# Four of 28 node spans: aggregate by gathered rows in the first graph layer as well

## The reference

```python
x0 = x
for l in range(3):                               # GRU layers
    m   = x @ weight[l]
    agg = segment_sum(m[src] * edge_weight[:, None], dst, 6250)
    x   = gru_cell(agg, x, w_ih, w_hh, b_ih, b_hh)
x = layernorm(x0 + x); x1 = x
for W, b in ((W0, b0), (W1, b1), (W2, b2)):      # GIN layers, no weights
    x = relu((x + segment_sum(x[src], dst, 6250)) @ W.T + b)
return layernorm(x1 + x)
```

## Time and profile before

| | us |
|---|---|
| median of 3 runs | 2881.55 |
| the profiled execution | 2883.43 |
| its span in the profile | 2881.7 |
| building stage up to PE's last unit | 993 |
| building stage and tail, up to layer 2's first transposes | 1014.5 |
| layers 2 and 3 up to the GIN layers | to about 2060 |

### The profile page before, as it was taken

One profiled execution on the slowest core, in us unless ns is written; L12 is line 12 of the kernel. 1 busy time (PEld: TensorE's weight loads), 2 busy tenths in 40 slices (PEclk: granted clock), 3 DMA queues, 4 the chain that ended last, 5 costly groups with the idle time before them and its releaser, 6 DMA issues.

```text
span 2881.7 us, 72532 instructions
## 1 busy us (share of the span) xinstructions
PE 2832.6 (98%) x29387; PEld 1881.3 (65%) x29387; DVE 1246.0 (43%) x2716; ACT 947.4 (33%) x1891; POOL 872.5 (30%) x1007
## 2 busy tenths in 40 slices
PE   6999999999999999999999999999999999999998
PEld 5899999999999955555555555555655555555554
DVE  7678877777888514344422344343500010001011
ACT  6777777777777610000001011101400010001111
POOL 4344344443444315554541454544000000000000
PEclk7999999999999999999999999999999999999999
DMA  5666666666662398998996988988487868886884
GB/s 196 267 262 244 245 261 261 257 241 251 262 263 95 113 397 342 350 339 326 355 369 253 340 338 331 357 330 327 149 326 301 310 248 301 309 304 247 318 304 163
DMA packets 134009, 810.64 MB, mean 281 GB/s; under 512 B 17208, under 2 KB 27308, under 8 KB 113948
## 3 DMA queue, kind: packets, MB, share of 16 engines
q1 hardware_dynamic: 111228, 758.32, 67.9%
q0 software_dynamic: 19968, 40.46, 4.4%
q10 hardware_dynamic: 2720, 10.62, 0.9%
HBM read 553.01 MB, written 256.33 MB: 281 GB/s over the span
## 4 chain that ended last, share of the span: by engine, by line
PE 95%; issue 2%; DVE 1%; ACT 1%; DMA 1%; another core or an unknown queue 0%; POOL 0%; DVEq 0%; SPq 0%; ACTq 0%; POOLq 0%
PE ps L969 29%; PE ps L1165 27%; PE ps L1247 19%; PE ps L1240 11%; PE ps L979 1%; PE ps L980 1%; PE ps L1260 1%; PE ps L1261 1%; PE ps L982 1%; PE ps L981 1%; PE ps L1144 1%; ACT ring L1661 0%; DMA sum_rows<-ring 0%; PE ps L1266 0%; PE ps L1267 0%
## 5 line engine op out<-in xcount | busy, mean ns | idle before, releaser
L969 PE MATMUL ps<-ring,Y 128*128 128x448 f32 x2352 | 888.4, 539 | 0.0
L1165 PE MATMUL ps<-ring,Y 128*128 128x448 f16 x4116 | 780.6, 352 | 0.0
L1661 ACT ACTIVATE ring<-ps 128x490 f16<-128x490 f32 (+1 forms) x1344 | 698.3, 651 | 176.7 <-PE ps L1240 169.1
L969 PEld LDWEIGHTS ps<-ring,Y 128*128 128x128 f32 x2352 | 446.4, 190 | 434.8 <-issue 434.8
L1165 PEld LDWEIGHTS ps<-ring,Y 128*128 128x128 f16 x4116 | 402.7, 98 | 373.8
L863 POOL DMA_INDIRECT ring<-y_rows,ring x448 | 431.4, 963 | 518.9 <-PE ps L969 257.7
L1247 PE MATMUL ps<-ring,Y 128*128 (+1 forms) x2744 | 570.2, 360 | 0.4 <-ACT shared L1620 0.4
L1247 PEld LDWEIGHTS ps<-ring,Y 128*128 128x128 f32 x2744 | 503.6, 190 | 8.4 <-ACT shared L1620 0.8
L1240 PEld LDWEIGHTS ps<-shared 64*128 64x128 bf16 x18816 | 320.4, 93 | 76.6 <-issue 59.3
L1240 PE MATMUL ps<-shared 64*128 64x49 bf16 (+1 forms) x18816 | 346.5, 189 | 20.0 <-issue 9.6
L1824 DVE TENSOR_SCALAR ring<-ring 128x128 f32<-128x128 f32 x446 | 130.9, 294 | 388.7 <-DMA ring<-y_rows,ring 205.0
(11 more groups left out here) (196 smaller groups left out, 1450.6 us busy)
## 6 DMA issues: line engine op xcount, KB each, us to landing
ring<-adj_w SPq DMA_DIRECT2D x72, 2688.0 KB
ring<-adj_h SPq DMA_DIRECT2D x42, 2800.0 KB, 9.4
ring<-adj_h SPq DMA_DIRECT2D x42, 2688.0 KB, 9.2
adj_w<-ring SPq DMA_DIRECT2D x48, 2016.0 KB, 11.9
adj_h<-ring SPq DMA_DIRECT2D x56, 1372.0 KB, 5.4
ring<-adj_w SPq DMA_DIRECT2D x24, 2912.0 KB
adj_w<-ring SPq DMA_DIRECT2D x48, 728.0 KB, 6.8
sum_rows<-ring SPq DMA_DIRECT2D x62, 448.0 KB
```

The lines of the kernel that those rows point to most:

```text
L969: mm = pe.matmul(ps[:, bank, 0:GW], Y[:, h, :], slab(s)[:, :, h - h0, :], start=(h == 0), stop=(last and h == TILES - 1))
L1165: mm = pe.matmul(ps[:, par, 0:GW], part[:, h, :], counts_slab(par, s)[:, :, h - h0, :], start=(h == 0 and part is Y_high), stop=(h == TILE ...
L1661: act.activation(strip[:, :, c0:c0 + UNIT * WIN].rearrange("p h (d j) -> p d h j", d=WIN)[:, :, :, w0:w1], psum_unit(a)[:, :, kind, :, :]. ...
```

## The change

The four last spans are no longer aggregated through `add_tiles` in the first GRU layer but by gathered rows, as in layers 2 and 3, during the building.

- Their slots come first (`ORDER`), build counts only (one matmul of three, one eviction of two, two column steps of seven) and have no `add_tiles`. PE's transposes of the inputs move from slots 0 and 1 to slots 1 and 2. The first gates run in slot 6 instead of slot 2.
- In slots 5 to 24 POOL gathers 224 rounds of rows of `x` (11 a slot, 12 in every fifth), ACT multiplies each by the weight two batches later, DVE adds it to the running sum two further batches later, SP stores four rounds at a time between the strips. The 16 row buffers are used in place; before there were 10 for rows and 14 for sums. Slots 26 and 27 fetch the 16 ends.
- Each group of gathers on POOL starts with `batch_begun`, a wait for the first unit of the batch and a `sem_inc`. The near rows are fetched at batch 2 instead of 7, the edge gathers wait for the first unit of batch 3 and 5 instead of the last unit of batch 2 and 4.
- After the last slot PE has the last strip's 49 tiles in six parts, with the gates of five spans between them (before: of one).
- The loops of DVE, ACT, POOL and SP over the slots are written out; the descriptor memory of POOL's DMAs is set to 8192.

```diff
+FIRST_RUN = GATHERS - RUN_SPANS
+ORDER = [*range(FIRST_RUN, GATHERS), *range(FIRST_RUN)]
+GATE_ORDER = [*range(FIRST_RUN - 1), *range(FIRST_RUN, GATHERS), FIRST_RUN - 1]
+SCALE_LAG, SUM_LAG, STORE_LAG = 2, 4, 5
+TAIL_TILES = [0, 6, 15, 24, 33, 42, TILES]
+RUN_SLOTS = range(RUN_SPANS + 1, GATHERS - 3)
+BATCH_ROWS = [2, 2, 1, 1, 2, 1, 0, 2]
-        KEYS_AT, STEPS_AT, LEAPS_AT = 2, 3, 5
+        KEYS_AT, STEPS_AT, LEAPS_AT = 2, 3, 0
-        NEAR_AT = 7
+        NEAR_AT = 2
...
+            def fetch_round(turn, i):
+                if i >= RUN_BUFS:
+                    if i % STORE == 0:
+                        use, q = divmod(i // STORE - STORE_TURNS, STORE_TURNS)
+                        pool.wait_ge(s_stored[q], stored_by(turn, q) + 16 * (use + 1))
+                    pool.wait_ge(s_acc, RUN * turn + i - RUN_BUFS + 2)
+                pool.indirect_dma_start(out=run_bufs[:, i % RUN_BUFS, :], ..., in_=y_rows if turn else x, ...)
+            def batch_begun(n):
+                pool.wait_ge(s_bmm, UNITS * (BUFS + n) + 1)
+                pool.sem_inc(s_mark_pool, 1)
+            def fetch_batch(n):
+                if rounds_at(n) or ends_at(n):
+                    batch_begun(n)
+                for i in rounds_at(n): fetch_round(0, i)
+            def prepare_span(t):
+                fetch_batch(n)
+                pool.wait_ge(s_key, ...); pool.wait_ge(s_colp, t + 1); pool.sem_inc(s_mark_pool, 1)
+                add_own(t + 1, 1 - par)
+                fetch_batch(n + 1)
+                near_rows(t + 3, 1 - par)
+                batch_begun(n + NEAR_AT)
+                gather_near(1 - par)
+                fetch_batch(n + 2)
+                take_places(t + 2, par)
+                batch_begun(n + FETCH_AT[0])
+                gather(par, 0)
+                fetch_batch(n + 3)
+                fetch_batch(n + 4)
+                batch_begun(n + FETCH_AT[1])
+                gather(par, 1)
+                fetch_batch(n + 5)
+                make_columns(t + 1, 1 - par, n + 6)
+                fetch_batch(n + 7)
...
+            def scale_rows(n):                       # ACT, after the evictions of batch n + 2
+                for i in rounds_at(n):
+                    act.wait_ge(s_row[i % RUN_BUFS], 16 * (i // RUN_BUFS + 1))
+                    act.activation(row, row, ACT.Copy, scale=run_edges[:, i, 1:2])
...
+                    sum_batch(n - SUM_LAG)           # DVE, after the one-hots of batch n
...
+            for c, n in enumerate(range(FIRST_RUN - 2, GATHERS)):     # PE, the tail
+                add_tiles(0, TAIL_TILES[c], TAIL_TILES[c + 1])
+                if n < GATHERS - 1:
+                    fused_gates(n)
+                if c < RUN_SPANS:
+                    flip_run(c)
```

More of the change, by code:

```diff
@@ L81 @@
 SPAN = WIN * LANES
+RUN_SLOTS = range(RUN_SPANS + 1, GATHERS - 3)
+BATCH_ROWS = [2, 2, 1, 1, 2, 1, 0, 2]
+MORE_AT, MORE_EVERY = 6, 5
+SLOT_ROWS = [[n + (k == MORE_AT and s % MORE_EVERY == 0) for k, n in enumerate(BATCH_ROWS)] for s in range(len(RUN_SLOTS))]
+assert sum(map(sum, SLOT_ROWS)) == RUN
+ENDS = 2 * WIN * RUN_SPANS
 STRIP_BATCHES = SUB // WIN // BATCH
@@ L844, in _ @@
[L844 to L847 removed]
+            def fetch_round(turn, i):
[4 more added lines that the diff above has]
+                    pool.wait_ge(s_acc, RUN * turn + i - RUN_BUFS + 2)
+                pool.indirect_dma_start(out=run_bufs[:, i % RUN_BUFS, :], out_offset=None, in_=y_rows if turn else x,
+                                        in_offset=bass.IndirectOffsetOnAxis(ap=run_edges[:, i, 0:1].bitcast(I32), axis=0))\
+                    .then_inc(s_row[i % RUN_BUFS], 16)
@@ L849, in _ @@
+            for t in range(GATHERS):
+                prepare_span(t)
             pool.wait_ge(s_steps, WIN * (GATHERS + 2))
@@ L1234, in build_unit @@
                             sums = psum_unit(a)[:, d, :, w - w0, :]
-                            if part == 0:
+                            if not weighted:
+                                rhs = hot[slots, buf, 0, w, 0:TILES]
+                                sums = sums[:, 0, :]
+                            elif part == 0:
                                 rhs = hot[slots, buf, 0:2, w, 0:TILES]
@@ L1251, in add_tiles, with flip_run, state_of @@
                         mm.then_inc(s_fagg, 1)
+            def flip_run(r):
+                n = GATE_ORDER.index(FIRST_RUN + r)
+                pe.wait_ge(s_joined, r + 1)
+                pe.wait_ge(s_fev, START + n)
+                for d in range(WIN):
+                    at = d * LANES
+                    mm = pe.matmul(ps[:, RUN_BANK, at:at + LANES], run_bufs[0:LANES, end_buf(r, d, 0), :],
+                                   ident[0:LANES, 0:LANES], start=True, stop=True)
+                mm.then_inc(s_fagg, 1)
+            def state_of(n):
+                span = GATE_ORDER[n] if isinstance(n, int) else n
+                return xT[:, bass.ds(span * SPAN, SPAN)]
             def fused_rz(n, bank):
-                xg = xT[:, bass.ds(n * SPAN, SPAN)]
+                xg = state_of(n)
                 pe.wait_ge(s_fev, START + n + 1)
@@ L1808, in rounds_by, with sum_row, sum_batch @@
                 return max(0, min(RUN, SLOT_FIRST + SLOT_NEXT * slot))
+            def sum_row(turn, i):
+                done = RUN * turn + i
+                row, last = (run_bufs[:, j % RUN_BUFS, :] for j in (i, i - 1))
+                dve.wait_ge(s_acc, done)
+                dve.wait_ge(s_prod, done - turn)
+                dve.scalar_tensor_tensor(out=row, in0=last, scalar=run_edges[:, i, 2:3], in1=row,
+                                         op0=ALU.mult, op1=ALU.add).then_inc(s_acc, 1)
+            def sum_batch(n):
+                for i in rounds_at(n):
+                    if i:
+                        sum_row(0, i)
             def add_rows(layer, slot, part=range(SLOT_NEXT)):
@@ L2091, in first_columns @@
                 rest = batches(2)
-                for p in range(WPARTS):
+                for p in range(WPARTS if has_weights(0) else 0):
                     part = columns[:, 0, :, 2 + p, :, :]
```

558 lines of the change are left out of this document (303 added, 255 removed).

## The result

| | us, median | lowest to highest | runs |
|---|---|---|---|
| before | 2881.26 | 2879.49 to 2884.94 | 9 |
| after | 2889.52 | 2886.71 to 2892.49 | 9 |

Ratio 1.0028, 95% interval 1.0019 to 1.0037: slower by 8.3 us, more than the 5.8 us that this measurement tells from no change. The forecast was 2920, slower by 38.5. The sign and the range held; the size was 30 us off, and the cause of the loss was not the one forecast. The same file is faster than the kernel before on another chip (third set), so the sign was luck as well.

What follows compares the result with a forecast made beforehand. PE was taken to bound the building stage at 34.2 us a slot; -62.5 us off PE plus 101 us of late columns behind POOL gave +38.5 on 2883.4, 2922, as a median 2920; range 2826 to 2938.

Steps and rivals of the forecast that it cites:

- The saved time: PE's building stage and tail: slot 5 starts at 135, tail 33 us, end at 952 against 1014.5, so -62.5 us.
- ACT and DVE: Scalings add 3.4 us a slot to ACT, sums 3.9 to DVE; both covered, costing nothing by themselves.
- POOL's 35.0: POOL in an 11-round slot: column steps done 35.0 us after PE's first unit, next slot at 38.6 instead of 34.2.
- the +101: Sum of building-stage losses from late columns: 4.4 us in each of 20 slots, plus twelfth rounds and slot 26.
- The price of a gather beside DVE: POOL's building-stage gathers, held up by DVE, take 1.29 us each instead of 0.95.
- The second price: Gap on POOL ahead of a gather behind a wait with `sem_inc`: 0.84 us for eight groups a slot.
- +0.83 count, +2.7 one-hots: DVE after the last column step: a count of 0.83 us and three one-hots of 2.7 before PE's next slot.
- rival two: POOL's gathers held up, but 0.84 paid only after a real wait or another instruction kind: slots 36.3, 2872; chance 0.10.
- Rival one: POOL's gathers not held up by DVE (1.0 each) but keeping their 0.84: slots 35.4, 2853; chance 0.15.
- The forecast's own range: Whole kernel at 2903 to 2937, from slot 5's start and slots of 37.8 to 39.4; chance 0.42.
- The layers kept their pace: Layers 2 and 3 keep pace and chain of ends; smaller stores and in-place buffers within 5 us, taken as nothing.
- some us more or less: Written-out loops: nothing could price them, so some us either way.

Runs made afterwards that it cites:

- third set: Four kernels on chip 11, the kernel before beside them; the changed kernel, unaltered, took 2849.52 us there, ratio 0.9896.
- e1: Changed kernel with layer 1's 224 gathers replaced by POOL clearing the same buffer, chip 10: 2826.59 us, ratio 0.9818.
- e17: The kernel of e15 once more, on chip 14: 2835.69 us, ratio 0.9853.
- e18: The kernel of e16 once more, on chip 14: 2834.60 us, ratio 0.9848.
- e9: The changed kernel, unaltered, once more on chip 11: 2849.52 us, ratio 0.9896 to the kernel before.
- e6: Changed kernel without layer 1's scalings on ACT; sums, gathers and stores stay; chip 5: 2892.98 us, ratio 1.0043.
- e14: Kernel before with two spare gathers a slot behind batch 0's last unit, read by nobody, on chip 7: 2909.97 us, ratio 1.0100.
- e13: The changed kernel, unaltered, once more on chip 7: 2891.01 us, ratio 1.0032 to the kernel before.
- e4: Kernel before with two spare gathers a slot behind batch 0's last unit, read by nobody, on chip 10: 2880.71 us, ratio 1.0005.
- e15: Changed kernel with column steps ahead of batch 5's edge gather (moved to batch 6), rounds redistributed and begun in slot 4; chip 7: 2879.45 us, ratio 0.9999.
- e16: Changed kernel with only POOL's column steps moved ahead of the second edge gather and batch 5's round; chip 7: 2901.01 us, ratio 1.0066.
- e8: Changed kernel with every building-stage group of gathers begun behind its batch's last unit, not the first; chip 5: 2915.64 us, ratio 1.0113.
- first two sets: Sets on chips 10 and 5, four kernels each with the kernel before beside them: gathers, scalings or sums left out, spare gathers, moved work.

## Why the prediction was right or wrong

**The saved time was right.** Slot 5's first added tiles are at 136.41; less the 2.9 us that two batches of units take in a full slot, it counts as started at 133.5 (forecast 135). The tail took 32.3 us (33). 1015.84 less the 64 us of losses is about 952 (952). That is a subtraction; `e1`, which has no gathers of rows at all, has its first transposes of layer 2 at 957.1, so the term is 57 to 63 us (62.5). `e17` and `e18` end the stage at 965.1 and 966.0: their slots with rounds lose nothing, but slot 5's tiles start 4.5 to 4.9 us later than in `e9` (141.1 and 141.5 for 136.6), with one wait of 10.9 us for DVE ahead of it; the rest I did not take apart. Slot 25, without rounds, is 34.3.

**ACT and DVE: right.** A scaling takes 437 ns, not 300, and by `e6` it is covered. Sums take 361 (352), and DVE's own time stays inside the slot. Group by line, 170 to 900 us (count, busy, mean ns, idle before):

```profile
L898 POOL DMA_INDIRECT run_bufs<-in_x,run_edges x212 | 258.6, 1220 | 138.9 <-PE ps L1333 93.9 <-issue 42.5 <-DVE shared L2213 0.3
L1768 ACT ACTIVATE run_bufs<-run_bufs,run_edges 128x128 f32<-128x128 f32 x215 | 82.1, 437 | 0.0
L1960 DVE SCALAR_TENSOR_TENSOR run_bufs<-run_bufs,run_edges 128x128 f32<-128x128 f32 x216 | 77.9, 361 | 6.7 <-ACT run_bufs L1768 3.3
```

**The failed step is POOL's 35.0, and with it the +101.** Columns came at 31.4 us on the recorded chip, where PE lost 1.1 us to them between 170 and 940 us, and at 31.2 on chip 11. The price of a gather beside DVE was about right: 1.220 on average, where 1.29 was taken. The second price was not: I charged 0.84 ahead of each of eight groups, from one row with a real wait and one behind another kind of instruction. In the slot of `e9` five of the groups found their wait met and paid 0.30, which is 2.7 us less, and the one behind the copies paid 0.15, 0.7 less; the two behind an address step paid 0.95. The shorter gathers are another 0.7 by the mean, so these terms more than cover the way from 35.0 to 31.2. The rest of the formula (+0.83 count, +2.7 one-hots) was right to 0.1 us. So the mechanism exists where nothing stalls, but was sized at 4.4 us a slot where it is 0.8; rival two (held up, 0.84 only after a real wait) is the one that describes POOL, and it too had the slot 1.5 us too long (36.3 for 34.85). Rival one's 2853 is nearest to chip 11's 2849.5, for a reason that is not its own. The forecast's own range (2903 to 2937) holds neither result.

**What took its place was not among the rivals.** On the recorded chip PE was 36.5 us a slot by itself, so columns 31.4 us into the slot were in time. In some 50 of the 64 us PE had all that it needed and stood still beside a gather of POOL. Without these stops the same kernel is 1.0% faster than before (`e9`), so "slower" came true by luck: nothing in the forecast stands for what made it so. The trace of before could not hint at it: its edge gather ends at 192.13, ahead of the next units at 192.88, while PE has its long tiles, and at 1.54 us it is of the long kind. The Trainium skill (SBUF — State Buffer, "Who interferes with whom") says, of access to SBUF, that PE never waits on another engine. The 0.43 and 0.47 us breaks here are waits without any releaser in the profile, and `e14` ties them to POOL's gathers; so either no SBUF port is behind them or the rule has an exception on some chips; no run tells which.

**The rest.** The layers kept their pace: layer 2's first product starts 1.4 us later than before, the last one of GIN 0.8 us. Behind that one, 12.6 us go by to the end of the program for 10.0 before. Every run of the changed kernel's form that I compared has this (12.3 to 12.8 us in `e1`, `e9`, `e13` and `e17`), and those of the kernel before with spare gathers do not (10.1 and 10.3 in `e14` and `e4`). So the change costs 2.5 us there that the prediction had at "some us more or less"; whether through the written-out loops or through the descriptor memory of 8192, no run tells.

**Left open.** What in a chip makes the stops. Four kernels were run on both kinds of chip (the changed one 2891.0 and 2849.5, the spare gathers 2910.0 and 2880.8, `e15` 2879.5 and 2835.7, `e16` 2901.0 and 2834.6), each chip in one set only, so a passing state of a chip isn't excluded. Why gathers that DVE holds up beyond 1.5 us rarely stop anything. That batch 5 loses little in the changed kernel fits this (13 of the 14 gathers that end in its units are such), and batches 6 and 7 have hardly an end in their units; but in `e8`, 19 of 19 short ends in batch 6 stop PE and only 1 of 18 in batch 5. And why the added tiles and layer 2, with matmuls of 0.2 us and more, show no such loss.

## What to carry over

A cost that the profile puts down to "issue" should be laid beside the ends of other engines' work, and the same file run on a second chip before one believes an account of it; comparing kernels across chips gave the wrong reading in the first two sets. Price a wait in its two cases, met and not met, from two separate rows. Where POOL issues gathers beside dense units of short matmuls, put what the next slot needs first (here the column steps), and let gathers end in long tiles (`e15` does both; the first alone, `e16`, was 10 us slower than the changed kernel on chip 7).

## What was not expected of the hardware

- A GpSimd indirect DMA of 128 rows stops TensorE, near the DMA's end or up to 0.7 us later, when TensorE is in a run of short matmuls (84 in 1.44 us). The profile shows 0.43 to 0.55 us idle; from start to start two matmuls are 0.6 to 0.7 us apart. It does so on chips 5 and 7 and in the recorded run, and not on chips 10, 11 and 14. Same kernel: 2889.5 and 2891.0 against 2849.5.
- A gather that ran longer than 1.5 us, held up by VectorE, had a stop beside it in 3 of 34 cases, a shorter one in 65 of 83 (recorded run).
- Several can come in a row: in slot 10 a unit stretch at 336.7 lost 3.56 us in five breaks 0.73 us apart, and in `e13` the same stretch lost 3.70. The first two of the recorded run:

```profile
336.71 1.48 PE L1333 MATMUL ps<-shared 64*128 64x98 bf16 x64
338.66 0.26 PE L1333 MATMUL ps<-shared 64*128 64x49 bf16 x4 [0.47 <-issue]
339.39 0.24 PE L1333 MATMUL ps<-shared 64*128 64x49 bf16 x4 [0.47 <-issue]
```

- The gap ahead of an indirect DMA is 0.30 us behind another one, also with a wait in between that is already met. It is 0.95 behind an instruction whose result GpSimd itself waits for, and 0.15 behind a copy that it doesn't wait for.
